# Two tiled sections a batch in place of three: weighings and sums moved beside mixing, a batch later

## The chip, the core and the metric

The kernel runs on one core of a Trainium2 chip. The metric is the device time of one execution in microseconds. Names of engines: PE is TensorE's matmuls and PEld its weight loads, DVE is VectorE, ACT is ScalarE, POOL is GpSimd, SP is SyncE, which issues the DMAs.

## What is computed

32 batches of 112 tokens of width 256 go through a cross attention (first half of the program) and then a feed-forward part that is itself an attention with switched experts (second half). The change is in the second half:

```python
def _L0_ffn_ref(x, Wq, Wk, Wv, Ws, Wd, Wo):          # H=16 heads, DH=64, E=8 experts, K=2
    q = jnp.einsum('btc,hdc->bhtd', x, Wq)
    k = jnp.einsum('btc,hdc->bhtd', x, Wk)
    gate_v = jnp.einsum('btc,hec->bthe', x, Ws)
    w, sel = jax.lax.top_k(gate_v, K)
    mix_v = jnp.einsum('bthk,bthke->bthe', jax.nn.sigmoid(w), jax.nn.one_hot(sel, E))
    proj_v = jnp.einsum('btc,edc->bted', x, Wv)
    v = jnp.einsum('bthe,bted->bhtd', mix_v, proj_v)
    probs = jax.nn.softmax(jnp.einsum('bhid,bhjd->bhij', q * scale, k), axis=-1)
    attn = jnp.einsum('bhij,bhjd->bihd', probs, v)
    gate_o = jnp.einsum('btc,hec->bthe', x, Wd)
    _, sel_o = jax.lax.top_k(gate_o, K)
    mask_o = jax.nn.one_hot(sel_o, E).sum(axis=3)
    return jnp.einsum('bthe,bthd,efd->bthf', mask_o, attn, Wo).sum(axis=2)
# x = x + tanh(g) * that, with x normalised over its width first
```

All of it is in float32.

## The kernel before

The second half is the function `switch`. Every engine has its instructions written out in a fixed order, a loop over the 32 batches b, and waits on semaphores; there is no scheduler. The steps of a batch, with the names that the profile shows:

- *Gates and experts.* `turn_x` (L1147) transposes the normalised x, `make_gates` (L1153) makes both sets of gates, `make_proj` (L1159) the values of all experts. On DVE `find_first` and `find_second` (L220 to L229) pick the two best experts, and `weigh_experts` (L1487 to L1494) puts the sigmoids of the gates beside the values in `pm`.
- *Mixing.* `pm` is stored to DRAM (`store_mix`, L1065) and loaded back in another layout as `pm_te` (`load_mix`, L1072). POOL spreads the weights into `mix_bd` (`spread_mix`, L1593), and `mix_values` (L1204) multiplies on 32x64 tiles of the array. The mixed values `mv` also go out and come back as `v` (`store_values` L1079, `load_values` L1085).
- *Attention.* `project` (L1167) makes queries and keys of a pair of batches, an eighth of them at a time: each such piece is called a fill, with 8 recorded matmuls, and there are four in a batch. `scores` (L1216) and `turn`, the transposition of the shifted scores (L1228), use 64 rows of the array for a matmul, two halves of it side by side; each handles half of the heads at a time. DVE takes maxima and subtracts (`shift`, L1499 and L1502), ACT takes exponentials into `probsT` (L1401).
- *Weighing and sums.* `weigh` (L1249) multiplies the turned probabilities with v on column tiles of 64. The last head of the second half does not fit its PSUM bank: its last 8 columns are made by `weigh_rest`, after a copy has freed the place. ACT copies the result to `att_q` (L1409, L1411), which goes out and comes back as `att_th` (`store_attention` L1091, `load_attention` L1097). DVE inverts the sums of probabilities (L1508), POOL spreads the picks of output experts (`spread_pick`, L1600 and L1604), and `sum_heads` (L1269, column tiles of 64) sums over heads.
- *Output.* The sums are copied to `uT` by DVE (`copy_lower_sums`, L1529) and ACT (`copy_upper_sums`, L1417), `output` (L1276) multiplies with the output weights, `residual` (L1536) adds to x, and SP stores the batch (L1115).

In pass b PE's order before is: mixing of b+1; turning and scores of b; fill; values of all experts of b+2; fill; turning of b and scores of b+1; transposes of x of b+4; fill; weighing of b and sums of b-1; gates of b+3; fill; output of b-1. A tiled section is a run of these steps that uses tiles of the array: mixing with turning and scores, then turning and scores, then weighing with sums. Everything else uses the full array. `probsT` holds one batch, both halves.

One pass of SP's order before:

```python
store_values(b + 1); store_mix(b + 2); load_values(b + 1); load_mix(b + 2)
store_attention(b); load_attention(b); store(b - 1)
```

Each of these waits for its own semaphores first, and those behind it wait with it. All DMAs of this half are on SP's queue.

Of the kernel before, what the change touches and what calls it, by code (L numbers as in the profile page):

```python
# [19 lines left out]
PSUM_BANK = 512  # L20
# [937 lines left out]
def switch(nc, z, d, c):  # L958
# [7 lines left out]
    with ExitStack() as ctx:  # L966
# [26 lines left out]
        probsT = sb("probsT2", [S, 2, 2 * G, S])  # L993
# [43 lines left out]
        ATT_COPIES = (2, 3)  # L1037
        ATT_BATCH = sum(ATT_COPIES)
        TAIL_AT, FITS = 2 * G * (S - D), PSUM_BANK - (2 * G - 1) * W


        def weighed(half, m):
            if m + 1 < 2 * G:
                return [(bank_g[:, half, m * W:(m + 1) * W], 0, W)]
            if half == 0:
                return [(bank_t[:, 1, TAIL_AT:TAIL_AT + W], 0, W)]
            return [(bank_g[:, 1, m * W:PSUM_BANK], 0, FITS), (bank_t[:, 1, TAIL_AT + W:TAIL_AT + 2 * W - FITS], FITS, W)]
# [9 lines left out]
        def _(sp):  # L1057
# [64 lines left out]
            for b in range(B):  # L1122
                if b + 1 < B:
                    store_values(b + 1)
                if b + 2 < B:
                    store_mix(b + 2)
                if b + 1 < B:
                    load_values(b + 1)
                if b + 2 < B:
                    load_mix(b + 2)  # L1130
                if b + 1 < B:
                    store_attention(b)
                    load_attention(b)
                else:
                    exchange_last()
                if b > 0:
                    store(b - 1)
# [4 lines left out]
        def _(pe):  # L1142
# [51 lines left out]
            def mix_values(b):  # L1194
                p, i = b % 2, b // 2
                pe.wait_ge(pm_loaded[p], 16 * i + 16)
                wait(pe, u_copied, 2 * (b - 2))
                wait(pe, att_copied, ATT_BATCH * (b - 1))
# [22 lines left out]
            def turn(b, half):  # L1221
                pe.wait_ge(shift_done, NG * b + 2 * half + 2)
                wait(pe, exp_done, 2 * (2 * b + half))
                wait(pe, att_copied, ATT_BATCH * b)
# [6 lines left out]
            def weigh(b, half):  # L1231
                p, i = b % 2, b // 2
                if half == 0:
                    pe.wait_ge(v_loaded[p], 16 * i + 16)
                pe.wait_ge(mv_copied, 2 * min(b + 2, B))
                wait(pe, att_copied, ATT_BATCH * b)
                final = b + 1 == B
                pe.wait_ge(exp_done, 4 * b + (2 if final and half == 0 else 4))
                for m in range(2 * G):
                    if final and half == 0 and m + 1 == 2 * G:  # L1240
                        pe.wait_ge(exp_done, 4 * b + 4)
                    last = weigh_head(b, half, m, weighed(half, m)[0])
                if half == 0:
                    last.then_inc(pv_done, 1)

            def weigh_head(b, half, m, place):
                dst, first, end = place
                for lo, hi in HALVES:
                    last = nc.tensor.matmul(dst[lo:hi, :], probsT[:, half, m, lo:hi], v[:, b % 2, 2 * G * half + m, first:end], start=True, stop=True)  # L1249
                return last  # L1250

            def weigh_rest(b):
                pe.wait_ge(att_copied, ATT_BATCH * b + ATT_COPIES[0])
                weigh_head(b, 1, 2 * G - 1, weighed(1, 2 * G - 1)[1]).then_inc(pv_done, 1)

            def sum_heads(b):
# [5 lines left out]
                pe.wait_ge(att_copied, min(ATT_BATCH * (b + 1) + 1, ATT_BATCH * B))  # L1262
# [33 lines left out]
            for b in range(B):  # L1296
                if 0 < b < B - 1:
                    mix_values(b + 1)
                if b + 1 < B:
# [4 lines left out]
                fill(b, 0)  # L1304
                if b + 2 < B:
                    if b == 0:
                        pe.wait_ge(xt_copied, 4)
                    wait(pe, out_done, b - 1)
                    make_proj(b + 2)
                fill(b, 1)  # L1310
                turn(b, 1)
                if b + 1 < B:
                    scores(b + 1, 0)
                if b + 4 < B:
                    pe.wait_ge(proj_copied, b + 3)
                    turn_x(b + 4)
                fill(b, 2)
                weigh(b, 0)
                weigh(b, 1)
                if b + 2 >= B:  # L1320
                    weigh_rest(b)
                if b > 0:
                    sum_heads(b - 1)
                if b + 2 < B:
                    weigh_rest(b)
                elif b + 2 == B:
                    turn(b + 1, 0)
                    scores(b + 1, 1)
                if b + 3 < B:
                    if b + 4 < B:  # L1330
                        pe.wait_ge(xt_copied, b + 5)
                    else:
                        pe.wait_ge(proj_copied, b + 3)
                    make_gates(b + 3)
                fill(b, 3)
                if b > 0:
                    if b + 3 < B:
                        pe.wait_ge(gates_copied, b + 4)
                    elif b + 2 < B:
                        pe.wait_ge(proj_copied, b + 3)  # L1340
                    else:
                        pe.wait_ge(out_done, b - 1)
                    output(b - 1)
            sum_heads(B - 1)
            pe.wait_ge(out_done, B - 1)
            output(B - 1)

        @block.scalar
        def _(act):
# [47 lines left out]
            def exps(b, half):  # L1397
                act.wait_ge(turned, 2 * b + half + 1)
                wait(act, pv_done, 2 * b + half - 1)
                for n, (lo, hi) in enumerate(HALVES):  # L1400
                    act.activation(probsT[:, half, :, lo:hi], bank_t[0:S, n, 0:2 * G * (hi - lo)].rearrange("s (m q) -> s m q", m=2 * G),  # L1401
                                   ACT.Exp).then_inc(exp_done, 1)

            def copy_attention(b, half):
# [5 lines left out]
                for src, at, end in weighed(half, 2 * G - 1):  # L1410
                    act.activation(att_q[:, b % 4, first + 7, at:end], src[0:S, :], ACT.Copy).then_inc(att_copied, 1)  # L1411
# [277 lines left out]
```

## Time and profile before

| | us |
|---|---|
| median of 3 runs | 1235.73 (1230.52 to 1237.83) |
| profiled execution | 1235.98 |
| its span | 1234.2 |
| PE busy in the span | 1177.5 (95%) |
| DVE busy | 870.7 (71%) |
| ACT busy | 643.0 (52%) |
| POOL busy | 549.3 (45%) |

The profiled execution's own time is 1.8 us longer than the span from its first instruction to its last. The second half runs from about 640 us to the end. Busy shares are means over stages; starts of instructions are measured, ends of matmuls are modelled, so gaps and steps are best read from starts. A releaser behind "<-" is the instruction or the transfer that ended a wait last.

### The profile page before, as it was taken

To read this page: it belongs to the slowest core of one execution; us is meant where nothing else is said; L and a number is where in the kernel's file an instruction comes from. 1 tells how busy PE (TensorE), PEld (TensorE's weight loads), DVE (VectorE), ACT (ScalarE), POOL (GpSimd) and SP (SyncE) were. 2 spreads that over 40 slices of the span, in tenths; PEclk is the share of its full clock that TensorE was granted. 3 is DMA by queue.
4 is the path that set the end of the run, shared out by engine and by line. 5 is a ranking of instruction groups with operands and counts; after the bars stand their busy time and mean duration, and the time that the engine had idled before them with its cause. 6 is when DMAs were issued, how large, how long until landed. Compare 5 with 4: busy or idle time off the path is not lost. (4 is left out here: it accounts for less than half of the span.)

```text
span 1234.2 us, 42190 instructions
## 1 busy us (share of the span) xinstructions
PE 1177.5 (95%) x16696; PEld 948.8 (77%) x16696; DVE 870.7 (71%) x2492; ACT 643.0 (52%) x1577; POOL 549.3 (45%) x821
## 2 busy tenths in 40 slices
PE   5699999999999999999879999999999999999985
PEld 4477777777777777777658888888888888888874
DVE  3477777777777777777665777677768767777753
ACT  3366666666666666666434444444444444444442
POOL 3476777777677677777610221221222122212110
PEclk9899999999999999999989999999999999999998
DMA  8999999888788778777405777676666757666773
GB/s 226 200 201 201 204 196 198 189 187 179 179 182 182 180 182 184 175 180 161 95 19 120 157 146 162 141 158 142 163 150 144 157 140 157 147 161 148 150 149 96
DMA packets 263012, 200.33 MB, mean 162 GB/s; under 512 B 195934, under 2 KB 243872, under 8 KB 258720
## 3 DMA queue, kind: packets, MB, share of 16 engines
q1 hardware_dynamic: 262816, 197.64, 72.7%
q8 instruction: 133, 2.18, 0.8%
q14 instruction: 63, 0.52, 0.2%
HBM read 125.49 MB, written 72.11 MB: 160 GB/s over the span
## 5 line engine op out<-in xcount | busy, mean ns | idle before, releaser
L899 POOL TENSOR_SCALAR shifted<-raw,neg_max 112x375 f32<-112x375 f32 x512 | 327.2, 648 | 164.4 <-DVE neg_max L781 120.8
L781 DVE CUSTOM_DVE_ANT_0 raw<-bank_s,maskb 112x375 f32<-112x375 f32 x512 | 266.5, 544 | 103.6 <-issue 88.1
L686 ACT ACTIVATE probsT<-bank_t 128x512 f32<-128x512 f32 (+3 forms) x512 | 189.1, 458 | 104.8 <-PE bank_t L460 104.8
L447 PE MATMUL bank_s<-K_stack,Q_stack 128*112 128x375 bf16 x512 | 150.8, 335 | 5.0 <-DVE neg_max L781 4.7
L460 PEld LDWEIGHTS bank_t<-ident,shifted 48*128 48x128 f32 (+1 forms) x3072 | 105.6, 139 | 28.1 <-issue 25.0
L460 PE MATMUL bank_t<-ident,shifted 48*128 48x48 f32 (+1 forms) x3072 | 122.8, 226 | 0.3 <-issue 0.3
L203 POOL TENSOR_SCALAR var_eps<-moments 112x1 f32<-112x1 f32 x32 | 7.2, 225 | 255.4 <-DVE moments L199 255.3
L1167 PE MATMUL bank_ab<-xnT,wq2T 128*128 128x224 f32 x512 | 109.5, 357 | 1.4 <-ACT kT L1383 0.6
L1167 PE MATMUL bank_ab<-xnT,wk2T 128*128 128x224 f32 x512 | 109.5, 357 | 0.0
L482 PE MATMUL bank_o<-probsT,V 128*32 128x112 f32 x3072 | 100.6, 263 | 5.0 <-ACT probsT L686 5.0
L1167 PEld LDWEIGHTS bank_ab<-xnT,wq2T 128*128 128x128 f32 x512 | 94.2, 190 | 12.3 <-issue 7.4
L1167 PEld LDWEIGHTS bank_ab<-xnT,wk2T 128*128 128x128 f32 x512 | 94.2, 190 | 10.3 <-issue 7.4
L1593 POOL TENSOR_TENSOR mix_bd<-pm_te,tok 128x448 f32<-128x448 f32 x32 | 30.1, 940 | 159.0 <-DMA pm_te<-pm_dram 159.0
L482 PEld LDWEIGHTS bank_o<-probsT,V 128*32 128x32 f32 x3072 | 69.5, 109 | 40.0 <-ACT probsT L686 26.1
L1499 DVE TENSOR_REDUCE max<-bank_s 112x4 f32<-112x448 f32 x128 | 78.8, 615 | 29.8 <-PE bank_s L1216 29.6
L414 PE MATMUL bank_ab<-ctxT,wk_sb 128*128 128x375 f32 x256 | 92.9, 487 | 0.9 <-ACT ctxT L646 0.9
L438 PE MATMUL bank_ab<-wv_sb,ctxT 128*128 128x256 f32 x372 | 90.8, 380 | 0.0
L447 PEld LDWEIGHTS bank_s<-K_stack,Q_stack 128*112 128x112 bf16 x512 | 63.0, 129 | 33.9 <-DVE neg_max L781 10.3
L1502 DVE TENSOR_TENSOR shifted<-bank_s,max 112x448 f32<-112x448 f32 x128 | 80.0, 625 | 4.4
L1529 DVE COPY uT<-bank_g 64x256 f32<-64x256 f32 x64 | 26.7, 417 | 77.7 <-PE bank_g L1269 77.3
L438 PEld LDWEIGHTS bank_ab<-wv_sb,ctxT 128*128 128x128 f32 x372 | 67.5, 190 | 6.5
L1375 ACT ACTIVATE qT<-bank_ab 128x448 f32<-128x448 f32 x64 | 34.8, 544 | 67.2 <-PE bank_ab L1167 67.2
(149 smaller groups left out, 2237.0 us busy)
## 6 DMA issues: line engine op xcount, KB each, us to landing
K_stack<-k_dram SPq DMA_DIRECT2D x64, 562.5 KB, 7.5
k_dram<-k_parts SPq DMA_DIRECT2D x32, 562.5 KB, 4.7
att_dram<-att_q SPq DMA_DIRECT2D x31, 511.0 KB, 3.3
att_th<-att_dram SPq DMA_DIRECT2D x31, 511.0 KB, 4.4
v_dram<-mv SPq DMA_DIRECT2D x32, 455.0 KB, 7.2
v<-v_dram SPq DMA_DIRECT2D x32, 455.0 KB, 4.5
K_stack<-k_dram SPq DMA_DIRECT2D x32, 375.0 KB, 9.3
Q_stack<-q_dram SPq DMA_DIRECT2D x64, 168.0 KB, 9.2
```

The lines of the kernel that those rows point to most:

```text
L414: last = nc.tensor.matmul(bank_ab[:, t, 0:S2], c.wk[:, e, t * P:(t + 1) * P], ctxT[:, p, e, 0:S2], start=(e == 0), stop=(e == EC - 1))
L438: last = nc.tensor.matmul(dst, ctxT[:, p, e, k * KP:(k + 1) * KP], c.wv[:, e, :], start=(e == 0), stop=(e == EC - 1))
L447: nc.tensor.matmul(bank_s[h % 2][0:S, 0:S2], Q_stack[:, p, h, :], K_stack[:, p, h, :], start=True, stop=True).then_inc(scores_ready, 1)
L460: return nc.tensor.transpose(bank_t[0:KP, bank, column:column + hi - lo], shifted[lo:hi, g % 2, j, k * KP:(k + 1) * KP], c.ident[lo:hi, lo ...
L482: last = nc.tensor.matmul(bank_o[j * VW:(j + 1) * VW, g * S:(g + 1) * S], V[:, p, k, G * g + j, :], probsT[:, g % 2, G * k + j, :], start= ...
L686: act.activation(probsT[:, g % 2, first_u:end, lo:hi], bank_t[0:KP, bank, column:column + (end - first_u) * (hi - lo)].rearrange("p (u q) ...
L781: dve.tensor_tensor_reduce(raw[:, g % 2, j, :], bank_s[h % 2][0:S, 0:S2], c.maskb[:, :], -1.0, -LEAST, ALU.add, ALU.min, neg_max[:, g % 2, ...
L899: pool.tensor_scalar(shifted[:, g % 2, j, 0:S2], raw[:, g % 2, j, :], -1.0, neg_max[:, g % 2, j:j + 1], ALU.mult, ALU.add).then_inc(shift_ ...
L1167: last = nc.tensor.matmul(bank_ab[:, 0, m * 2 * S:(m + 1) * 2 * S], w, xnT[:, e, 2 * h:2 * h + 2, :].rearrange("p r s -> p (r s)"), start= ...
L1375: act.activation(qT[:, h, 2 * f:2 * f + 2, :, :].rearrange("p m r s -> p (m r s)"), bank_ab[:, 0, 0:4 * S], ACT.Copy, scale=float(D) ** -0 ...
L1499: dve.tensor_reduce(neg_max[:, g % 2, :], sc, AXX, ALU.max).then_inc(max_done, 1)
L1502: dve.tensor_tensor(shifted[:, g % 2, :, :], sc, neg_max[:, g % 2, :].unsqueeze(2).to_broadcast([S, G, S]), ALU.subtract).then_inc(shift_d ...
```

## The change

Weighing of batch b-1 and sums of batch b-2 now stand in pass b right behind mixing, turning and scores, so that a pass has two tiled sections. `probsT` gets a second buffer, by b % 2. The last head of each half gets a place of its own in another PSUM bank (one in `bank_t`, one in `bank_ab`, or in the last batch elsewhere), so `weigh_rest` and one copy on ACT go. The copies, the residual, the picks, the stores and loads of attention move with these steps, on ACT, DVE, POOL and SP. The output of b-2 stands between the first two fills, the gates between the last two. Waits are set anew. The core of the diff:

```diff
-        probsT = sb("probsT2", [S, 2, 2 * G, S])
+        probsT = sb("probsT2", [S, 2, 2, 2 * G, S])
...
+                return bank_g[:, half, m * W:(m + 1) * W]
+            if half == 1:
+                return bank_t[:, 1, TAIL_AT:TAIL_AT + W]
+            return bank_ab[:, 0 if b + 1 == B else 1, 0:W]
...
@@ SP
                 if b + 1 < B:
                     store_values(b + 1)
+                if b > 0:
+                    store_attention(b - 1)
                 if b + 2 < B:
                     store_mix(b + 2)
                 if b + 1 < B:
                     load_values(b + 1)
+                if b > 0:
+                    load_attention(b - 1)
+                if b > 1:
+                    store(b - 2)
                 if b + 2 < B:
                     load_mix(b + 2)
-                if b + 1 < B:
-                    store_attention(b)
-                    load_attention(b)
...
@@ PE, the new pass
+                last_batch = b + 1 == B
                 if 0 < b < B - 1:
                     mix_values(b + 1)
+                if not last_batch:
                     turn(b, 0)
...
                     scores(b, 1)
+                if b > 0:
+                    weigh(b - 1, 0)
+                    weigh(b - 1, 1)
+                if b > 1:
+                    sum_heads(b - 2)
...
                     make_proj(b + 2)
+                fill(b, 0)
+                if b > 1:
...
+                    output(b - 2)
                 fill(b, 1)
                 turn(b, 1)
...
                     scores(b + 1, 0)
...
                     turn_x(b + 4)
                 fill(b, 2)
-                weigh(b, 0)
-                weigh(b, 1)
...
                     make_gates(b + 3)
                 fill(b, 3)
...
+            weigh(B - 1, 0)
+            weigh(B - 1, 1)
+            for b in range(B - 2, B):
+                sum_heads(b)
+                pe.wait_ge(out_done, b)
+                output(b)
...
@@ POOL
+                if b + 2 < B:
+                    spread_mix(b + 2)
                 if b > 0:
                     spread_pick(b - 1)
-                if b + 2 < B:
-                    spread_mix(b + 2)
```

Three places show the order. On PE, before, from the sums at the end of the third section to the next mixing (matmuls in float32 are shown once here and recorded twice in a trace):

```order
L1269 MATMUL bank_g<-pick_bd,att_th 64x64 x14
L1249 MATMUL bank_t<-v,probsT 64x8
L1249 MATMUL bank_t<-v,probsT 48x8
L1153 MATMUL bank_ab<-wgT,xnT 112x256 x2
L1167 MATMUL bank_ab<-xnT,wk2T 128x224 x4
L1276 MATMUL bank_ab<-wo2T,uT 112x256 x4
L1204 MATMUL bank_g<-pm_te,mix_bd 64x64 x28
```

And on PE now, from the last head of weighing, in the first section of a pass, on:

```order
L1252 MATMUL bank_t<-v,probsT 64x65
L1252 MATMUL bank_t<-v,probsT 48x65
L1272 MATMUL bank_g<-pick_bd,att_th 64x64 x14
L1159 MATMUL bank_ab<-wv2T,xnT 112x512 x2
L1167 MATMUL bank_ab<-xnT,wq2T 128x224 x4
L1279 MATMUL bank_ab<-wo2T,uT 112x256 x4
L1167 MATMUL bank_ab<-xnT,wq2T 128x224 x4
```

The two narrow matmuls are gone, the values of all experts follow the sums, and the output stands between two fills.

On SP, one pass before, from the store of mixed values on:

```order
L1079 DMA v_dram<-mv 128x14x65
L1065 DMA pm_dram<-pm 112x640
L1085 DMA v<-v_dram 112x1040
L1072 DMA pm_te<-pm_dram 128x7x80
L1091 DMA att_dram<-att_q 112x1168
L1097 DMA att_th<-att_dram 128x14x73
L1115 DMA out_dram<-X 112x256
```

And now:

```order
L1078 DMA v_dram<-mv 128x14x65
L1090 DMA att_dram<-att_q 112x1168
L1064 DMA pm_dram<-pm 112x640
L1084 DMA v<-v_dram 112x1040
L1096 DMA att_th<-att_dram 128x14x73
L1114 DMA out_dram<-X 112x256
L1071 DMA pm_te<-pm_dram 128x7x80
```

The load of `pm_te` went from the place behind the load of v to the end of the pass, behind the load of attention and the store of the output.

On DVE now, from the last subtraction of a pass's first pair of shifts to its residual (before, the moments L197 and L199 stood ahead of L1487, and the copies L1529 behind the next pair of shifts):

```order
L1512 TENSOR_TENSOR shifted<-bank_s,max 112x448
L1539 COPY uT<-bank_g 64x4x64 x2
L1497 TENSOR_SCALAR sig<-sig 112x32
L1498 RECIPROCAL sig<-sig 112x32
L1500 TENSOR_TENSOR mix_part<-one_hot,sig 112x128 x2
L1504 TENSOR_TENSOR pm<-mix_part 112x16x8
L197 BN_STATS stats<-X 112x6
L199 BN_AGGR moments<-stats 112x2
L211 TENSOR_SCALAR xn<-X,moments,rstd 112x256
L1546 SCALAR_TENSOR_TENSOR X<-bank_ab,tanh_g,X 112x256
```

The copy of the lower sums now stands ahead of the weights of the experts, the moments and the residual behind them.

## Rows read from the trace of the kernel before

**Rows 1.** Busy time by engine, 28 passes; then clock, DMA share, GB/s
```profile
693.78:1194.90 501.12, 499.26 (x7433) 426.45 (x7432) 364.42 (x886) 236.49 (x584) 106.24 (x136) 1.00 0.69 151
```

**Rows 2.** Timeline of PE, one pass: start, us, instructions, count, idle before
```profile
873.00 1.04 PE L1204 MATMUL bank_g<-pm_te,mix_bd 32*64 32x64 f32 x56
...
875.39 1.78 PE L1167 MATMUL bank_ab<-xnT,wq2T 128*128 128x224 f32 x8
877.01 1.88 PE L1159 MATMUL bank_ab<-wv2T,xnT 128*112 128x512 f32 x4
878.72 1.68 PE L1167 MATMUL bank_ab<-xnT,wq2T 128*128 128x224 f32 x8
880.33 0.65 PE L1228 MATMUL bank_t<-ident,shifted 64*112 64x64 f32 x16
...
881.99 1.69 PE L1167 MATMUL bank_ab<-xnT,wq2T 128*128 128x224 f32 x8
883.62 1.03 PE L1249 MATMUL bank_g<-v,probsT 112*64 112x65 f32 x28
...
886.63 1.12 PE L1153 MATMUL bank_ab<-wgT,xnT 128*112 128x256 f32 x4
887.59 1.68 PE L1167 MATMUL bank_ab<-xnT,wk2T 128*128 128x224 f32 x8
889.10 1.89 PE L1276 MATMUL bank_ab<-wo2T,uT 128*112 128x256 f32 x8
890.92 0.28 PE L1204 MATMUL bank_g<-pm_te,mix_bd 32*64 32x64 f32 x4
```

**Rows 3.** Timeline of DVE and ACT, around the mixing at 890.92
```profile
886.74 0.85 DVE L1529 COPY uT<-bank_g 64x256 f32<-64x256 f32 x2 [2.42 <-PE bank_g L1269]
...
888.20 0.38 ACT L1359 ACTIVATE gates<-bank_ab 112x256 f32<-112x256 f32 x1
888.68 0.42 DVE L220 TENSOR_REDUCE best<-gates 112x32 f32<-112x256 f32 x1 [1.09 <-ACT gates L1359]
...
891.43 0.48 DVE L1536 SCALAR_TENSOR_TENSOR X<-bank_ab,tanh_g,X 112x256 f32<-112x256 f32 x1
...
896.70 0.42 DVE L197 BATCH_NORM_STATS2 stats<-X 112x6 f32<-112x256 f32 x1
...
897.25 0.15 DVE L1487 TENSOR_SCALAR sig<-sig 112x32 f32<-112x32 f32 x1
...
898.35 0.39 DVE L1494 TENSOR_TENSOR pm<-mix_part 112x128 f32<-112x128 f32 x1
```

**Rows 4.** Timeline of SP's DMA issues in the same pass
```profile
898.81 0.30 SPq L1065 DMA_DIRECT2D pm_dram<-pm  x1
900.01 0.30 SPq L1085 DMA_DIRECT2D v<-v_dram  x1
901.34 0.38 SPq L1072 DMA_DIRECT2D pm_te<-pm_dram  x1
```

**Rows 5.** Timeline of POOL in the same pass
```profile
905.36 0.94 POOL L1593 TENSOR_TENSOR mix_bd<-pm_te,tok 128x448 f32<-128x448 f32 x1 [4.22 <-DMA pm_te<-pm_dram]
```

**Rows 6.** Columns as rows 1, a stretch with the attention load alone
```profile
892.00:894.00 2.00, 2.00 (x36) 1.89 (x37) 1.86 (x5) 1.97 (x5) 0.00 (x0) 1.00 1.04 226
```

**Rows 7.** DMA issues from 649.9 to 650.6 us: count, KB, us to landing
```profile
pm_te<-pm_dram SPq DMA_DIRECT2D x1, 280.0 KB, 2.8
```

**Rows 8.** Line L1072, the load of pm_te, over 28 passes
```profile
DMA to landing us min/median/max: 3.0/4.3/5.6
```

**Rows 9.** Timeline of PE and SP at the end of the program
```profile
1194.90 1.04 PE L1204 MATMUL bank_g<-pm_te,mix_bd 32*64 32x64 f32 x56
...
1204.41 1.12 PE L1269 MATMUL bank_g<-pick_bd,att_th 128*64 128x64 f32 x28 [0.49 <-issue]
...
1213.48 0.74 SPq L1106 DMA_DIRECT2D att_dram<-att_q  x2
...
1219.01 1.94 PE L1269 MATMUL bank_g<-pick_bd,att_th 128*64 128x64 f32 x28 [6.38 <-issue]
```

More of the change, by code:

```diff
@@ L1223, in turn @@
                 wait(pe, exp_done, 2 * (2 * b + half))
-                wait(pe, att_copied, ATT_BATCH * b)
+                wait(pe, att_copied, ATT_BATCH * (b if half == 1 or b + 1 == B else b - 1))
                 for m in range(2 * G):
@@ L1234, in weigh @@
                     pe.wait_ge(v_loaded[p], 16 * i + 16)
[L1235 to L1238, printed above, removed]
-                for m in range(2 * G):
[L1240 to L1254, printed above, removed]
+                if b + 2 < B:
+                    pe.wait_ge(mv_copied, 2 * (b + 2) + half + 1)
+                else:
+                    pe.wait_ge(u_copied, 2 * (b - 1))
+                    pe.wait_ge(att_copied, ATT_BATCH * b)
+                pe.wait_ge(exp_done, 4 * b + 2 * half + 2)
+                for m in range(2 * G):
+                    if m + 1 == 2 * G:
+                        if half == 1:
+                            pe.wait_ge(exp_done, 4 * b + (6 if b + 2 < B else 4))
+                        elif b + 1 == B:
+                            pe.wait_ge(kk_copied, 4 * (B // 2))
+                        elif b + 3 < B:
+                            pe.wait_ge(gates_copied, b + 4)
+                        else:
+                            pe.wait_ge(out_done, b - 1)
+                    for lo, hi in HALVES:
+                        last = nc.tensor.matmul(weighed(b, half, m)[lo:hi, :], probsT[:, p, half, m, lo:hi], v[:, p, 2 * G * half + m, :], start=True, stop=True)
+                last.then_inc(pv_done, 1)
             def sum_heads(b):
@@ L1303, in _ @@
                     scores(b, 1)
-                fill(b, 0)
+                if b > 0:
[3 more added lines that the diff above has]
+                    sum_heads(b - 2)
+                if last_batch:
+                    turn(b, 0)
+                    scores(b, 1)
                 if b + 2 < B:
@@ L1307, in _ @@
                         pe.wait_ge(xt_copied, 4)
-                    wait(pe, out_done, b - 1)
+                    else:
+                        pe.wait_ge(att_copied, ATT_BATCH * (b - 1) + 2)
                     make_proj(b + 2)
+                fill(b, 0)
+                if b > 1:
+                    if b + 2 < B:
+                        pe.wait_ge(proj_copied, b + 3)
+                    else:
+                        pe.wait_ge(att_copied, ATT_BATCH * (b - 1) + 2)
+                    output(b - 2)
                 fill(b, 1)
                 turn(b, 1)
-                if b + 1 < B:
+                if not last_batch:
                     scores(b + 1, 0)
                 if b + 4 < B:
-                    pe.wait_ge(proj_copied, b + 3)
+                    if b > 1:
+                        pe.wait_ge(out_done, b - 1)
+                    else:
+                        pe.wait_ge(proj_copied, b + 3)
                     turn_x(b + 4)
                 fill(b, 2)
-                weigh(b, 0)
-                weigh(b, 1)
[L1320 to L1323, printed above, removed]
-                if b + 2 < B:
[L1325 to L1328, printed above, removed]
                 if b + 3 < B:
@@ L1409, in copy_attention @@
                 act.activation(att_q[:, b % 4, first:first + 7, 0:W], bank_g[0:S, half, 0:7 * W].rearrange("s (m w) -> s m w", w=W), ACT.Copy).then_inc(att_copied, 1)
-                for src, at, end in weighed(half, 2 * G - 1):
-                    act.activation(att_q[:, b % 4, first + 7, at:end], src[0:S, :], ACT.Copy).then_inc(att_copied, 1)
+                act.activation(att_q[:, b % 4, first + 7, 0:W], weighed(b, half, 2 * G - 1)[0:S, :], ACT.Copy).then_inc(att_copied, 1)
             def copy_upper_sums(b):
```

99 lines of the change are left out of this document (45 added, 54 removed).

## Prediction

> **What bounds the kernel now.** I read the page first, then the second half by stretches, then one of its batches engine by engine. From 693.78 to 1194.90 us TensorE counts as busy for 499.26 of 501.12 us at a granted clock of 1.00, and the DMA engines for 0.69 [rows 1]. That stretch is 28 batches of 17.90 us. "Busy" alone proves little, since matmul ends are modelled, but the starts within a batch [rows 2] leave no hole: each group starts where the group before it runs out, and the next mixing comes 17.92 us after the last. So in the steady state TensorE's own order sets the time, and everything else has slack. Two things have to be seen: what a step costs TensorE, and how much slack the longest side path has, which is the path from the gates to the mixing of a later batch.
>
> What a switch costs is seen in the projections of [rows 2], 8 recorded matmuls each. Between full-array work one takes 1.51 us (887.59 to 889.10). After scores it takes 1.62 (875.39 to 877.01), before turning 1.61, before weighing 1.63. So entering a tiled section costs about 0.10 to 0.12, and leaving one about 0.11 that falls on the first full-array group.
>
> **The side path before.** I count from the start of a mixing, M (890.92 in this batch). VectorE starts the selection at 888.68, M-2.24, when the gates are copied [rows 3], works through both selections, two score shifts and the weights of the experts, and ends the piece of pm at 898.35+0.39, M+7.82. SyncE stores pm at 898.81, loads v at 900.01 and pm_te at 901.34 [rows 4]. GpSimd starts mix_bd at 905.36, and it is ready 0.94 later, at M+15.4 [rows 5]. The next mixing is due at M+17.92, so the slack is 2.5 us.
>
> **The change, part by part.**
> 1. *TensorE per batch.* Mixing, turning and scores stay at 2.39. Weighing and sums took 3.01 for some 96 recorded matmuls, 31 ns each; the four narrow ones of the remainder go: -0.12. The projection that stood before weighing no longer enters a tiled section: 1.63 to 1.51. The gates no longer follow one: 0.96 to 0.86. The projection before mixing now enters one (1.51 to 1.61) and the output no longer does (1.82 to 1.72). The first group behind the sums is now proj (1.71 to 1.81), and the projection after it is relieved (1.62 to 1.51). In order: 2.39+2.89+1.81+1.51+1.72+1.61+1.66+1.51+0.86+1.61 = 17.57; I take 17.6, or -0.3 a batch.
>  How often the array's tiling changes is a second way to count: 7 times a batch before (full, mixing, turning, full, turning, full, weighing, full), 6 times now, since scores to weighing remains a change. At 0.11 a change and with the remainder that is -0.23. The Trainium skill (TensorEngine Tiling (Array Packing), Key Properties) has it that a change of the tiling mode, not of the tile, drains TensorE; it supports this second count, by which the batch would take 17.7.
> 2. *Turned probabilities in two buffers, copies.* No instruction is added; a weighing a batch later only finds its exponentials ready sooner. The copies on ScalarE and VectorE are the same, less one: nothing on the path. Covers that I checked: weighing begins at M+2.4 and its targets are freed by the copy of the mixed values; the tail that shares a bank with the turned scores waits for exponentials that end well before its turn. If ScalarE were late there, TensorE would wait by as much.
> 3. *The path to mixing.* Three things move on it.
>  (a) The gates now stand one projection ahead of mixing, not a projection and an output: 0.86+1.61 = 2.47 before M. Their last matmul ends 1.12 after their start [rows 2], ScalarE is free (before, the copy of sums held it until 888.20) and needs 0.48 to VectorE's start [rows 3]: M-0.82, so 1.4 later against M than before.
>  (b) On VectorE the residual (0.48) and the moments (0.55) leave the stretch between selection and pm, the copy of the lower sums (0.85) comes in [rows 3]: 10.06 becomes 9.9. The store of pm goes out at M+9.15, not M+7.89.
>  (c) SyncE's order. Before, pm_te was loaded right after v. Now the attention load (511 KB) and the output store (112 KB) go out between v and pm_te. SyncE itself loses nothing (the residual is done near M+11.4), but the transfers share one queue. In the stretch where the attention load runs alone the engines are full, 1.04 at 226 GB/s [rows 6], so 623 KB hold the queue for 2.75 us. That a transfer waits for the one ahead is seen in [rows 7, 8]: an early pm_te load, alone, landed 2.8 us after its issue, while behind v it takes 4.3 (median; 3.0 to 5.6). The Trainium skill (DMA: Bandwidth & Descriptors, Queues, rings and completion order) says that on each DMA engine descriptors are consumed in ring order; the 2.8 against 4.3 agrees with that.
>  From the store of pm to mix_bd took 6.55 before. Now it is 6.55+2.75, less some 0.5, because v is stored well before pm now and its load follows the pm store at once (0.9 at most; nothing at least). So mix_bd starts at M+9.15+8.8 = M+17.95 and is ready at M+18.9. TensorE is there at M+17.6: **1.3 us late**. Bounds: the queue 20% faster and the full saving give about 0.2 late; the slowest landing of [rows 8] gives 2.6.
>  (d) The wait does not add up in full. The gates stand ahead of it, so a stall s brings the selection, and with it the pm store, s earlier against the next mixing. The lateness of one batch is shared by two: s is about half, 0.65 (0.1 to 1.0, the top held down because the load of v cannot go before v's store has landed). The batch takes 17.6+0.65 = **18.25**, 0.35 longer than 17.90: 28 x 0.35 = +9.8.
> 4. *Start and end.* At the start the weighing of a batch falls out of the first pass and the passes are short; in the last steady pass TensorE has no gates to do but still waits for mix_bd. I set these against each other at 0, plus or minus 2. The tail: before, from the last mixing at 1194.90 to the end are 39.3 us, and the sums of batch 29 start 9.5 in [rows 9]. Now those sums need an attention exchange that starts 5 us after that mixing, queues behind the stores and loads of v, and ends in the two steps of picks on GpSimd: about 17.5 in, with nothing for TensorE to do from 11.6 on. From these sums to the last exchange took 9.1 before (1204.41 to 1213.48), and from there to the end 20.7, of which the sums and output of batch 30 (6.7, from 1219.01 on) can now partly lie inside the exchange: 16 to 20.7. So 42.6 to 47.3; I take 44, **+4.5**.
>
> **The sum.** The profiled execution took 1235.98 us (span 1234.2), the median of the runs is 1235.73, so they can stand for each other. 1235.98+9.8+4.5 = 1250.3. **I predict 1250 us, slower.** The bounds: s = 0.1 gives 17.7 and 1235; s = 1.0 gives 18.6, +19.6, and a tail of +7 gives 1262.
>
> **The rivals.**
> - *The load is in time* (the other side). If pm_te lands by M+16.6, because the transfers overlap more than I allow or the pm store goes out earlier, TensorE never waits. For it: the slack before was 2.5 us. Against it: 1.26 of that goes with the store, 0.3 with the shorter batch, and the transfers ahead would have to cost under 1. It decides at a lateness of 0. Then 28 x -0.3 = -8.4 and the tail +4.5: 1232; with a tail of only +2, 1229.5. By the count of tiling changes (-0.2 a batch) it is 1235.
> - *Gain and wait cancel.* A lateness of 0.5 to 0.7 gives a stall near 0.3 and the old 17.9: 1235 to 1241. For it: the lower bound of 3c. Against: every slow landing of v or pm_te goes on the path now.
> - *The attention load is what comes late.* VectorE inverts its sums just ahead of the next selection. If the load lands after M+16 it delays the selection, and the stall no longer shortens the path: 18.6 a batch, 1258. For it: the load stands behind v; against: I get it landed near M+15.5.
> - *That the change is not carried out* is excluded: the order shows weighing and sums behind scores, in place of after the third projection.
>
> **How the numbers follow.** A measurement of this kernel can tell about 0.5% from no change, so 1229.6 to 1241.9 counts as the same. Forecast, a stall that costs more than the switches save (with the late attention load as its far end): 0.60, nearly all slower. Cancelling: 0.20, the same. In time: 0.20, half of it under 1229.6. So faster 0.10, same 0.30, slower 0.60. The range goes from the no-stall case to s = 1.0 with the long tail: 1230 to 1263.
>
> **What the new profile would show.** Right: GpSimd's mix_bd starting about 18 us after a mixing with the pm_te load as its releaser, TensorE idle 0.4 to 1 us ahead of each mixing, the batch near 18.25, TensorE's work between two waits near 17.6, and the sums of batch 29 some 17 us after the last mixing. Wrong: mix_bd ready before the projection ahead of mixing ends (then the batch reads 17.6 to 17.7), an idle TensorE ahead of sums or proj in place of mixing, or a projection before the gates that still takes 1.6.

## The result, and the profile after

The changed kernel takes 1287.97 us (median of 4 runs, 1286.43 to 1293.2), the kernel before 1234.24 in the same comparison: a ratio of 1.0439, interval 1.041 to 1.0468. It is **slower by 4.4%**, where +1.2% was forecast, and lies outside the range. The profiled execution took 1288.95, its span is 1287.1.

The 28 steady passes of the new kernel, as [rows 1] for the old one (columns: stretch, us, busy time of PE, PEld, DVE, ACT and POOL with instructions, granted clock, DMA share, GB/s); below it the end of the program, from the last mixing on:

```profile
688.28:1239.94 551.66, 503.31 (x7320) 431.12 (x7321) 408.27 (x888) 235.42 (x556) 112.69 (x137) 0.98 0.63 137
```
```profile
1239.94:1287.10 47.16, 31.63 (x504) 26.50 (x504) 14.78 (x32) 11.51 (x30) 6.17 (x6) 0.80 0.40 98
```

A pass takes 551.66 / 28 = 19.70 us against 17.90: +50.5. The end takes 47.2 against 39.3: +7.9. The stretch from the first mixing to the fourth is 2.1 shorter (42.02 against 44.09), and the first half of the program, which the change does not touch, was 3.4 shorter in this execution. Together +52.9, the whole difference of the spans.

What TensorE waited for in the same 28 passes (total us, times, longest), from the table of waits:

```profile
POOL mix_bd L1604 <- DMA pm_te<-pm_dram: 236.7, 28, 15.7
PE bank_g L1204 <- POOL mix_bd L1604: 45.6, 27, 3.2
DVE recip L1518 <- DMA att_th<-att_dram: 21.2, 25, 1.9
```

So it is the wait ahead of mixing, as forecast, but 1.63 a pass in place of 0.65. Seven of the 28 passes take 19.00 to 19.02 us, the others 18.55 to 21.64. One of the seven, called regular below, PE first, as [rows 2]:

```profile
845.75 1.04 PE L1204 MATMUL bank_g<-pm_te,mix_bd 32*64 32x64 f32 x56 [1.25 <-POOL mix_bd L1604]
...
848.14 1.03 PE L1252 MATMUL bank_g<-v,probsT 112*64 112x65 f32 x28
...
851.08 1.97 PE L1159 MATMUL bank_ab<-wv2T,xnT 128*112 128x512 f32 x4
852.89 1.68 PE L1167 MATMUL bank_ab<-xnT,wq2T 128*128 128x224 f32 x8
854.40 1.89 PE L1279 MATMUL bank_ab<-wo2T,uT 128*112 128x256 f32 x8
856.13 1.68 PE L1167 MATMUL bank_ab<-xnT,wq2T 128*128 128x224 f32 x8
...
861.79 1.71 PE L1167 MATMUL bank_ab<-xnT,wk2T 128*128 128x224 f32 x8
864.75 1.04 PE L1204 MATMUL bank_g<-pm_te,mix_bd 32*64 32x64 f32 x56 [1.25 <-POOL mix_bd L1604]
```

TensorE's own work is what was worked out: 19.00 - 1.25 = 17.75 (17.6 forecast, 17.7 by the count of tiling changes). SP's issues in that pass and the next store of pm, as [rows 4], and POOL around the next mixing, as [rows 5]:

```profile
851.01 0.32 SPq L1090 DMA_DIRECT2D att_dram<-att_q  x1
854.73 0.32 SPq L1064 DMA_DIRECT2D pm_dram<-pm  x1
855.14 0.38 SPq L1084 DMA_DIRECT2D v<-v_dram  x1
855.62 0.39 SPq L1096 DMA_DIRECT2D att_th<-att_dram  x1
856.96 0.45 SPq L1114 DMA_DIRECT2D out_dram<-X  x1
857.54 1.68 SPq L1071 DMA_DIRECT2D pm_te<-pm_dram  x1
...
873.74 0.32 SPq L1064 DMA_DIRECT2D pm_dram<-pm  x1
```
```profile
863.52 1.08 POOL L1604 TENSOR_TENSOR mix_bd<-pm_te,tok 128x448 f32<-128x448 f32 x1 [7.44 <-DMA pm_te<-pm_dram]
864.57 0.56 POOL L1611 TENSOR_TENSOR pick_s<-att_th,recip 128x112 f32<-128x112 f32 x1
865.21 1.79 POOL L1615 TENSOR_TENSOR pick_bd<-pick_s,tok 128x896 f32<-128x896 f32 x1
```

mix_bd starts at M+17.77 (17.95 forecast) and is ready at M+18.85 (18.9 forecast). What was not forecast is on DVE, as [rows 3], with ScalarE's copy of the gates ahead of it:

```profile
862.00 0.39 ACT L1365 ACTIVATE gates<-bank_ab 112x256 f32<-112x256 f32 x1 [0.32 <-PE bank_ab L1153]
...
862.25 0.24 DVE L1518 RECIPROCAL recip<-att_th 128x14 f32<-128x14 f32 x1 [0.52 <-DMA att_th<-att_dram]
862.48 0.42 DVE L220 TENSOR_REDUCE best<-gates 112x32 f32<-112x256 f32 x1
...
865.45 0.42 DVE L220 TENSOR_REDUCE best<-rest 112x32 f32<-112x256 f32 x1
865.90 1.38 DVE L221 TENSOR_TENSOR tie<-rest,best 112x256 f32<-112x256 f32 x1
...
873.28 0.38 DVE L1504 TENSOR_TENSOR pm<-mix_part 112x128 f32<-112x128 f32 x1
```

The reciprocal waits for the attention load, and the selection stands behind it. In this pass that costs nothing, since the gates are copied only at 862.39; in most others the load lands later (M+16.78 in the median, M+16.48 here). And one operation, tie<-rest,best, takes 1.38 us instead of 0.43; it ends 0.28 after pick_bd. By line, over the 28 passes (duration in ns, minimum/median/maximum), before and after:

```profile
L221 DVE TENSOR_TENSOR tie<-rest,best x28: 424/426/428, 695.1 to 1179.2; 112x256 f32<-112x256 f32 x28
```
```profile
L221 DVE TENSOR_TENSOR tie<-rest,best x28: 424/1382/1848, 691.7 to 1222.1; 112x256 f32<-112x256 f32 x28
```

### The profile page after: what moved, and what is told of

The parts are those of the page before. It is cut to its first block, busy times and chain, and to the rows that moved or that the text cites. A ratio compares the mean times of both kernels' runs of the same rounds, so it can differ in the third digit from the quotient of the medians.

```text
span 1287.1 us, 41844 instructions
## 1 busy us (share of the span) xinstructions
PE 1184.2 (92%) x16568; PEld 955.2 (74%) x16568; DVE 914.6 (71%) x2492; ACT 641.7 (50%) x1545; POOL 555.8 (43%) x821
## 4 chain that ended last, share of the span: by engine, by line
DVE 14%; issue 12%; PE 12%; DMA 9%; POOL 2%; SPq 1%; ACT 1%; POOLq 0%; DVEq 0%; ACTq 0%
DMA att_th<-att_dram 7%; PE bank_ab L1167 3%; DVE tie L221 2%; DVE one_hot L224 2%; DMA att_dram<-att_q 2%; PE bank_g L1252 2%; DVE max L1509 2%; PE bank_s L1216 2%; DVE tie L222 1%; DVE first_tie L223 1%; PE bank_ab L1279 1%; DVE best L220 1%; DVE uT L1539 1%; PE bank_g L1204 1%; PE bank_t L1228 1%
## 5 line engine op out<-in xcount | busy, mean ns | idle before, releaser
L460 PEld LDWEIGHTS bank_t<-ident,shifted 64*128 64x128 f32 (+1 forms) x3072 | 105.4, 139 | 27.8 <-issue 24.5
L447 PEld LDWEIGHTS bank_s<-K_stack,Q_stack 128*112 128x112 bf16 x512 | 63.1, 130 | 34.4 <-DVE neg_max L781 10.8
L1389 ACT ACTIVATE kT<-bank_ab 128x448 f32<-128x448 f32 x64 | 34.8, 544 | 93.6 <-PE bank_ab L1167 93.6
L1204 PE MATMUL bank_g<-pm_te,mix_bd 32*64 32x64 f32 x1792 | 35.4, 228 | 49.6 <-POOL mix_bd L1604 49.4
```

What stands on the lines that cost most here:

```text
L447: nc.tensor.matmul(bank_s[h % 2][0:S, 0:S2], Q_stack[:, p, h, :], K_stack[:, p, h, :], start=True, stop=True).then_inc(scores_ready, 1)
L460: return nc.tensor.transpose(bank_t[0:KP, bank, column:column + hi - lo], shifted[lo:hi, g % 2, j, k * KP:(k + 1) * KP], c.ident[lo:hi, lo ...
L1204: last = nc.tensor.matmul(bank_g[col:col + D, n // 2, k * D:(k + 1) * D], mix_bd[row, k, :, :].rearrange("p t h -> p (t h)"), pm_te[row, p ...
```

## The experiments

The chain of waits around that pass (start, us, what) names two DMAs ahead of the selection, though the gates come no earlier in it:

```profile
845.75 1.04 PE bank_g L1204 x56
...
850.27 0.55 ACT att_q L1415
...
851.01 4.59 DMA att_dram<-att_q
...
855.62 6.61 DMA att_th<-att_dram
...
862.25 0.18 DVE recip L1518
...
865.90 1.39 DVE tie L221
```

I began with three theories. **A**: a ring of mix_bd, the picks behind it on GpSimd, VectorE held by them, pm, its store and load, and mix_bd again. **B**: the late attention load, ahead of the selection. **C**: the queue alone, pm_te behind the attention load. Three edits of the changed kernel cut one link each; they were run alone, in pairs and together.

**Load order (L): pm_te ahead of the attention load.**
```
                 if b + 1 < B:
                     load_values(b + 1)
+                if b + 2 < B:
+                    load_mix(b + 2)
                 if b > 0:
                     load_attention(b - 1)
                 if b > 1:
                     store(b - 2)
-                if b + 2 < B:
-                    load_mix(b + 2)
```


> The pm_te load is issued right behind the v load, ahead of the attention load and the output store. Three theories. C (the queue alone: pm_te waits behind the attention load): pm_te lands 2 us earlier, mix_bd is ready before TensorE comes, a pass is 17.6 to 17.9 us, the whole 1230 to 1240. A (a ring: mix_bd, then the picks on GpSimd, which hold up VectorE's selection, then pm, its store and load, mix_bd again): the attention load is now issued some 2 us later and lands near 17.5 us after a mixing, so the reciprocal, the picks and with them the selection come later; the ring from one pm store over the attention load (2.8 us to its issue, 5.5 to land), the reciprocal (0.25) and VectorE's 11.2 us to the next pm store is 19.7 us, so 19.5 to 20 a pass, 1283 to 1300. B (the late attention load alone holds the selection, the picks cost nothing): the same place, with VectorE at 10.0: 18.5 to 19, 1255 to 1270.

Measured: 1323.78 us, ratio 1.0699 (1.0662 to 1.0736), 20.73 a pass. C falls. pm_te does land 4.1 us after its issue in place of 5.9, but the attention load is issued later:

```profile
DVE recip L1518 <- DMA att_th<-att_dram: 77.1, 28, 3.6
PE bank_g L1272 <- ACT att_q L1416: 50.7, 28, 2.5
PE bank_g L1204 <- POOL mix_bd L1604: 9.9, 19, 1.4
```

These are the waits of that run. VectorE's reciprocal now waits in every pass. The second line is a result of that: ScalarE's exponential of the gates needs the second selection and stands ahead of the copies of the attention, on which the sums wait. In that run it starts 5.65 us after a mixing (2.81 in the change, both medians), and the copies start 0.13 to 0.14 behind it in every pass. The wait moved; it did not go. A had the direction, but the time is 24 us over its range.

**Reciprocal (R): behind the first selection.**
```
+                if b + 3 < B:
+                    select_first(b + 3)
                 if b > 0:
                     invert_sums(b - 1)
-                if b + 3 < B:
-                    select_first(b + 3)
```


> VectorE inverts the sums behind the first selection instead of ahead of it, so that a late attention load no longer holds the selection. B (late attention load): the selection starts with the gates, a pass is about 18.3 us, the whole near 1262. A (ring with the picks): the picks come later, about 3 us after the selection's start, and hold the second selection until some 0.3 us after their end: pm is stored 1 us later, 19.5 to 19.9 a pass, 1285 to 1305; the operation held is still tie<-rest,best, now near 2 us. C (queue alone): no change, within 5 us of 1288.

Measured: 1309.6 us, ratio 1.0597 (1.0554 to 1.064), 20.03 a pass, 5 us above A's range. B alone falls: with the selection free of the load, the picks come later and hold its second half. The held operation is not tie<-rest,best but mostly the next one, tie<-tie,rank_w, up to 1.84 us.

**No picks (N).**
```
+                if b > 0:
+                    size = [P, 1, 8, X]
-                pool.tensor_tensor(pick_bd[:, :, :, :], pick_s[:, :, :]...
+                pool.tensor_tensor(pick_bd[:, 0:size[1], :, :], pick_s[:, 0:size[1], :]...
```


> From the second batch on GpSimd writes one of the 14 groups of pick_bd, so the op that ran 1.79 us takes some 0.2 (this leaves the other groups' picks out of the result). A: VectorE's tie<-rest,best falls from 1.38 to 0.43 us, the stretch from best to pm from 11.2 to about 10.1, a pass to 18.4 to 18.7, the whole to 1250 to 1260. B: the attention load still holds the selection, so the passes that were longer than 19.0 stay, 1265 to 1280. C: no change, 1283 to 1293.

Measured: 1281.03 us, ratio 1.0356 (1.0315 to 1.0397), 19.09 a pass: a miss of A by 21 us. The operation did what A said (its line in that run, as above):

```profile
L221 DVE TENSOR_TENSOR tie<-rest,best x28: 424/425/428, 700.6 to 1213.9; 112x256 f32<-112x256 f32 x28
```

But not all of an earlier pm reaches mix_bd. In the pass whose mixing starts at 833.65, SP and POOL show why:

```profile
841.68 0.32 SPq L1064 DMA_DIRECT2D pm_dram<-pm  x1
...
843.54 0.38 SPq L1096 DMA_DIRECT2D att_th<-att_dram  x1
...
845.71 1.12 SPq L1071 DMA_DIRECT2D pm_te<-pm_dram  x1
```
```profile
850.75 0.94 POOL L1604 TENSOR_TENSOR mix_bd<-pm_te,tok 128x448 f32<-128x448 f32 x1 [7.71 <-DMA pm_te<-pm_dram]
```

pm's store goes out 0.95 earlier (M+8.03), but the attention load still goes at M+9.89, when its own store has landed, and pm_te stands behind it: mix_bd starts at M+17.10, 0.67 earlier. Over all passes, VectorE's stretch from the start of the selection to the store of pm is 1.0 shorter in the mean (10.62 against 11.65), but the selection still waits for the attention load in many passes: it starts at M+17.14, against M+17.38.

**All three (L, R, N).**


> The edits of the three other runs together: pm_te load right behind the v load, reciprocal behind the first selection, one of 14 groups of pick_bd (the other groups' picks are left out). If queue, late attention load and held selection are all there is, TensorE sets the pass again: 17.6 to 17.7 us, mixing never waits, and with the start 5.5 us shorter and the tail 7.9 longer than in the kernel before the whole is 1226 to 1236. If there is a fourth cause, passes stay above 18.2 and the whole above 1248.

Measured: 1241.03 us, ratio 1.0026 (1.0001 to 1.0051). That is 5 us above the range for the three being all there is, and 7 below the bound for a fourth cause. TensorE sets the pass again in half of the batches, at 17.69 (its steady passes, columns as above):

```profile
690.80:1193.87 503.07, 494.08 (x7321) 423.70 (x7321) 376.71 (x889) 234.90 (x557) 69.25 (x136) 1.00 0.71 150
```

The mean is 17.97 (5.6 us of waits ahead of mixing, 10 times), so the three links together are worth the 47 us between this run and the change. 17.69 is TensorE's own pass: 0.2 below the old one, not 0.3.

**The pairs.** L and R, with the picks whole:

> Two of the three edits, with the picks kept whole: pm_te load ahead of the attention load, reciprocal behind the first selection. Against the run with all three edits (1241) it shows what the picks cost once load order and selection are freed. Held selection counts (ring theory): the picks then run about 2 to 4.6 us after a mixing, beside the second selection, and VectorE's tie<-rest,best is held near 2 us; the sums wait for them until 4.6; 18.5 to 19.1 a pass, 1260 to 1280. Held selection costs nothing: within 5 us of 1241.

Measured: 1269.2 us, ratio 1.0271 (1.0237 to 1.0305), 18.86 a pass. Against 1241 the picks cost 28 us. The held operation of that run:

```profile
L222 DVE TENSOR_TENSOR tie<-tie,rank_w x56: 424/1474/1842, 690.9 to 1203.9; 112x256 f32<-112x256 f32 x56
```

R and N, with the load order of the change:

> Reciprocal behind the first selection and one of 14 groups of pick_bd (the other groups' picks are left out), with the load order of the change. What is left is the pm_te load behind the attention load, which cannot go before the attention store has landed 10 us after a mixing: attention load lands near 16, pm_te near 17, mix_bd ready near 18.2. If that queue is a cause of its own: 18.1 to 18.5 a pass, 1250 to 1262. If the queue costs nothing once the selection is free: within 5 us of 1241.

Measured: 1280.8 us, ratio 1.036 (1.0331 to 1.0389), 19.28 a pass: 40 us for the load order alone, where I had put 9 to 21. L and N, with the reciprocal ahead of the selection:

> pm_te load ahead of the attention load and one of 14 groups of pick_bd (the other groups' picks are left out), the reciprocal still ahead of the selection: the last cell of the three edits. If the late attention load holds the selection by itself: the ring from one pm store over the attention load (3.1 us to its issue, 5.7 to land), the reciprocal (0.25) and VectorE's 10.5 us to the next pm store is 19.5 us, 19 to 19.6 a pass, 1268 to 1290. If held picks were all that mattered once the load is early: 1238 to 1250.

Measured: 1283.99 us, ratio 1.0389 (1.0367 to 1.0411), 19.46 a pass, as the ring over the attention load says: 43 us for that link alone.

| edits made | us | edits made | us |
|---|---|---|---|
| none (the change) | 1288.0 | L, R | 1269.2 |
| L | 1323.8 | L, N | 1284.0 |
| R | 1309.6 | R, N | 1280.8 |
| N | 1281.0 | L, R, N | 1241.0 |

Each link that is left in costs 28 to 43 us by itself; no single cut brings more than 7, and two make it worse.

**Queue or bytes?** The pm_te load on ScalarE's queue, without and with R:
```
-    (SyncE)  if b + 2 < B: load_mix(b + 2)
     (ScalarE, per batch)
     copy_fill(b, 1)
+    if b + 2 < B: load_mix(b + 2)
     exps(b, 1)
```


> The change as it is, but the pm_te load is issued by ScalarE, on a queue of its own, some 12.7 us after a mixing. If pm_te is late because it stands behind the attention load in SyncE's queue, it now lands within 4 us of its issue, mix_bd is ready near 17.5, and a pass is 17.7 to 18.2 us, the whole 1232 to 1248. If it is late because the DMA engines are full with the attention load, or because the late attention load holds the selection, the queue does not matter: 18.8 or more a pass, 1270 to 1295.

> The pm_te load on ScalarE's queue, and the reciprocal behind the first selection, picks whole. If queue and late attention load are the causes: 17.7 to 17.9 a pass, 1232 to 1242. If the held second selection still counts by itself: 18.2 to 18.8, 1250 to 1270.

Measured: 1303.6 us, ratio 1.0541 (1.0511 to 1.0571), and 1307.39 us, ratio 1.0586 (1.0543 to 1.0628). Both miss. From issue to landing of pm_te, in the change and in the first of these:

```profile
DMA to landing us min/median/max: 4.6/5.9/7.4
```
```profile
DMA to landing us min/median/max: 4.6/6.0/6.9
```

A queue of its own does not bring it sooner. It was issued later, since it has to find its place among ScalarE's copies (in the median 13.0 after a mixing, 12.1 in the change), and ScalarE now waited for pm's store, 7.4 us in 9 passes. That may account for part of the 16 us by which the first of them is longer than the change; the rest, and the second run, stay open.

The bytes, in the run with R and N: the attention load cut to 7 of its 14 groups, then only the output store moved behind the pm_te load.
```
-    att_th[:, p, :, :]       <- rows(att_dram, b, AW)
+    att_th[:, p, groups, :]  <- rows(att_dram, b, AW)[:, groups, :]    (7 of 14 from b = 2)
```


> The run with the reciprocal behind the selection and one of 14 groups of pick_bd, and from the third batch on the attention load brings 7 of its 14 groups (so the other groups' attention and picks are left out of the result): 256 KB fewer ahead of pm_te in the queue. If the bytes ahead of pm_te set its landing: at the 226 GB/s of [rows 6] pm_te lands 1.1 us earlier, and the selection freed of the attention load lets a pass fall from 18.9 to 17.8 to 18.3, 1245 to 1265. If SyncE's waits (attention store landed, residual done) set it, and the bytes do not: within 6 us of 1281.

Measured: 1256.04 us, ratio 1.0165 (1.0127 to 1.0202), 18.45 a pass: 25 us less than with the whole load. From the store of pm to mix_bd it now takes 8.08 us in the mean of the passes, 9.15 with the whole load: 1.07, where 1.1 was forecast.

```
+    load_mix(b + 2)
     store(b - 2)
-    load_mix(b + 2)
```


> The run with the reciprocal behind the selection and one of 14 groups of pick_bd (the other groups' picks are left out), with only the output store moved behind the pm_te load: SyncE no longer waits for the residual (issue at 11.1 to 12.6 us after a mixing) ahead of the pm_te load, and 112 KB fewer stand ahead of it. If that wait is what holds the pm_te load: its issue goes to 10.6 to 11.5, a pass to 18.0 to 18.4, 1255 to 1268. If the landing of pm's store and the attention load ahead hold it: 0.3 us a pass or less, 1272 to 1284.

Measured: 1273.81 us, ratio 1.0301 (1.0258 to 1.0343): 7 us less, but the two intervals overlap. From the store of pm to mix_bd takes 9.10 in the mean, as good as unchanged. So the bytes of the attention load count, and SyncE's wait for the residual shows no cost of its own.

**A version that takes the attention out of the way.** Sums and output stand one batch later still. Then the attention exchange goes behind the pm_te load again, and reciprocal and picks go ahead of VectorE's score shifts, behind the weights of the experts. The edit in short:
```
 (SyncE)   store_values(b+1), store_mix(b+2), load_values(b+1), load_mix(b+2),
           store_attention(b-1), load_attention(b-1), store(b-3)
 (TensorE, ScalarE, VectorE)
-    sum_heads(b - 2), output(b - 2), copies and residual of b - 2
+    sum_heads(b - 3), output(b - 3), copies and residual of b - 3
 (VectorE) normalise_x(b + 4)
+          invert_sums(b - 2)
-          invert_sums(b - 1) ahead of select_first(b + 3)
 (GpSimd)  inverse_deviation(b + 4)
+          spread_pick(b - 2)
           spread_mix(b + 2)
-          spread_pick(b - 1)
```


> The two tiled sections of the change, with the sums and the output one batch later still, so that the attention exchange goes back behind the pm_te load in SyncE's order (as in the kernel before), and the reciprocal and the picks run beside VectorE's score shifts, behind the weights of the experts. If the collision of the attention exchange with the exchanges of v and pm, and the held selection, are what cost the time: TensorE sets the pass at 17.7 (what it needed in the run with all three edits), mix_bd ready near 16.5, VectorE's two-input operations at 0.43; the start is shorter by one more sum, the tail longer by it; 1224 to 1240, so within 1% of the kernel before, on its faster side if anything. If the wait has another cause (the later gates alone): above 1250.

Measured: 1232.95 us over 12 runs, ratio **0.9963** (0.9947 to 0.998): 4% under the change, and the only version below the kernel before. Its steady passes, its waits ahead of mixing and the line of the held operation:

```profile
693.89:1190.55 496.66, 491.39 (x7286) 421.32 (x7285) 366.30 (x885) 234.24 (x555) 105.81 (x136) 1.00 0.67 152
```
```profile
PE bank_g L1204 <- POOL mix_bd L1608: 3.4, 4, 1.9
```
```profile
L221 DVE TENSOR_TENSOR tie<-rest,best x28: 424/424/426, 696.1 to 1175.7; 112x256 f32<-112x256 f32 x28
```

The passes take 17.74 (4.5 us less in all), the stretch from the first mixing to the fourth 2.1 less, the end 42.6 in place of 39.3. The picks are whole, and none holds a tie<-rest,best any more: in the pass that starts at 907.02 they run from 918.22 to 920.41, while VectorE has only its residual to do before the shift at 920.53.

## Why the prediction was wrong

The direction and the place of the wait were right; the size was not. By its steps:

1. *TensorE per pass.* Right: 17.75 in the pass shown, 17.69 in the runs that wait little. The second way to count, 17.7, was the better one. The single groups agree: 1.81 for the values of all experts behind the sums, 1.51 for the projection after them, 1.73 for the output (1.72). The Trainium skill (TensorEngine Tiling (Array Packing), Key Properties) has it that a change of the tiling mode drains TensorE, which supports that count; the trace agrees, by the 17.69.
2. *Copies at no cost.* Right: in 23 of the 28 passes the copies of the attention end 5.2 to 5.5 us after the mixing, and in four of the other five the granted clock was at its lower level for a stretch.
3. *The path to mixing.* (a) The selection starts 16.73 after the mixing before it, 16.78 forecast (17.6 - 0.82): right. Seen from the next mixing it is M-2.27 (862.48 against 864.75), since 1.25 of stall lie between. (b) From there to the store of pm takes 11.26, 9.97 forecast (M-0.82 to M+9.15): wrong. That pm still goes out at M+8.98 (9.15 forecast) is luck: the selection starts earlier by the stall, and takes longer by as much. (c) mix_bd starts 8.79 after that store, 8.8 forecast: right in this pass, 9.22 in the mean. That it is ready at M+18.85 (18.9 forecast) is the same luck. [rows 6] is not the attention load alone, as was read: the output store went out at 891.94 and the store of v at 893.04. The price of a byte held all the same, in the run with half the attention load.

**The step that failed is 3b**: VectorE's stretch from the selection to pm, taken from the kernel before and priced at 9.9 us. It put at nothing what GpSimd does meanwhile. Since the change the picks follow mix_bd at once, and both run beside the selection, whose operations with two inputs are held until they end. Beyond their shortest time the operations of lines 221 to 229 took 1.42 us a pass longer, summed over the 28 passes; in the kernel before 0.12, and with the picks cut (N) 0.48. With the other two links cut, the picks alone lengthen 1241.0 us to 1269.2. With 11.26 in place of 9.97 the forecast's own sum comes to 18.9 a pass and 1268 us, above its range.

Step 3d, that the stall is half of the lateness, held. Laid out in one line from a mixing over the gates, pm and mix_bd to the mixing after the next, the forecast is 16.78 + 9.97 + 8.8 + 0.94 = 36.5 in two passes, or 18.25 a pass. The regular pass has 16.73 to the selection, 11.26 to the store of pm, 8.79 to mix_bd and 1.23 to the mixing: 38.0, or 19.0. Two passes of TensorE's own work are 35.5, so without a stall mixing would come 2.5 late, and the stall of 1.25 is half of that. In the mean over the steady passes (27 such pairs) the four terms are 17.38, 11.65, 9.22 and 1.13, 39.4 in all, or 19.7 a pass. Of the 2.9 that the forecast lacks, 1.7 are VectorE's stretch, 0.6 the later selection, 0.4 the way from the store of pm to mix_bd and 0.2 the last term.

The later selection is in part my third rival (the late attention load): I took the load to be landed near M+15.5, and it lands at M+16.48 in the regular pass and M+16.78 in the median. In the regular pass the way over it, 5.26 from a mixing to the attention store, 11.22 for store and load and 0.25 for the reciprocal, reaches the selection just when the gates do: 16.73. The picks close a path of their own in one pass: 3.48 from the start of mix_bd to the end of the picks, 0.28 until the held operation ends, 6.46 to the store of pm and 8.79 to mix_bd, again 19.0.

So the waits are not one late transfer but several rings of nearly one length that share engines, and cutting one leaves the next; the runs fit that, since no single edit brought more than 7 us and all three together 47. I had priced the ring over the gates, but with VectorE's time from the kernel before, and did not lay out the other two.

Three slips in the sums change nothing here: 3a's terms give M-0.87, not M-0.82; the lower bounds of 3c leave a lateness of about 0.4, not 0.2; and a pass of 18.6 adds up to 1260, not 1258.

4. *Start and end.* The start came 2.1 shorter, at the edge of my 0 plus or minus 2. The end was +7.9, +4.5 forecast, just inside its upper bound of 47.3. The sums of batch 29 start 18.4 after the last mixing (17.5 forecast), after 5 us with an idle TensorE, and the granted clock of the end is 0.80 as against 0.87 before (means of the two levels, 1.2 and 2.4 GHz).

The sum of the steady passes, +9.8 forecast, was +50.5; the regular pass alone would make +30.8 of it (28 x 1.10). Counted at TensorE it is -5.9 for its shorter pass, +45.6 of waits ahead of mixing, and 10.8 that are left. Most of these are the clock: TensorE is busy for 503.31 us at a granted clock of 0.98, against 494.08 at 1.00 for the same instructions in the run with all three edits. In the change the clock was at 0.50 (1.2 GHz) in four stretches, 17.1 us together, each during a stall of 1.9 to 3.1 us ahead of a mixing or less than 2 us behind one. Five other stalls of that length in the steady passes were not followed by one. What makes single passes longer than the regular one beyond that is not shown. With a path that never stalls, the change could have been worth 0.2 us a pass, 6 us in all, which its longer end gives back.

## What to carry to other kernels

Where a step moves work a stage later, follow each wait around until it comes back to the instruction where it began, over as many passes as that takes, and divide. Price each link with what will run beside it after the move, not with its time before. When rings of nearly equal length share engines, a single cut shows little or makes it worse; try the cuts together once before dropping a theory. And a transfer that had the queue to itself for half a pass is not free to move: look at what it will then stand ahead of.

## What the runs showed of the hardware

A VectorE operation with two inputs in SBUF that comes while GpSimd runs one that reads SBUF is held: it ends 0.28 us behind GpSimd's (867.28 and 867.00 in the pass shown). The hold shows as a longer operation (tie<-rest,best 1.38 us in the median and up to 1.85, in place of 0.43), not as idle time, so no view of waits names it. Operations with one input are not touched (best<-rest, 0.42 with pick_bd beside it), nor are the shifts, which read PSUM: in the kernel before, 53 of them ran wholly inside a pick and took 0.61 to 0.63 us, like the others. The Trainium skill says so (SBUF — State Buffer, Who interferes with whom): a VectorE instruction with two SBUF inputs contends with a GpSimd instruction that reads SBUF, one with at most one SBUF input, outside the two-port modes, does not. The Trainium skill adds (SBUF — State Buffer, Summary: rules for kernel authors) that the second to issue then blocks until the first finishes. The trace agrees, and the page would have named the missing term of 3b.

A second queue did not let a load pass the one ahead: 6.0 us from issue to landing on ScalarE's queue, 5.9 on SyncE's, and in the median pm_te landed 1.2 us behind the attention load on the one and 1.3 on the other. The Trainium skill (DMA: Bandwidth & Descriptors, Issuing engines are not separate DMA queues) has it that DMAs of all engines run on the same 16 DMA engines and interleave there; the two medians agree. The order of issue did count: ahead of the attention load pm_te landed in 4.1 to 4.2 us.
